# Weight prefetches of a mixture-of-experts stage issued from the SyncE queue instead of the ScalarE queue

## The reference, cut to what matters

```python
xn = _layernorm(x)
x = x + attn(xn) + ffn(xn)

# attn: one head of width 2048
qkv = einsum('bsh,oh->bso', xn, w_qkv) + b_qkv
q, k, v = split(qkv, 3)
probs = softmax(q @ k.T / sqrt(H))
out = (probs @ v) @ w_out.T + b_out

# ffn: 8 experts of width 1024, all computed densely, and a shared one
ht = rmsnorm(xn) ; top-2 of softmax(ht @ router_w) gives w_dense [t, 8]
eo = (silu(ht @ w_gate[e]) * (ht @ w_up[e])) @ w_down[e]
moe = sum over e of w_dense[:, e] * eo
sh  = (silu(ht @ sw_gate) * (ht @ sw_up)) @ sw_down
```

## Time and profile before

| | us |
|---|---|
| median of the 2 timed runs | 6501.62 |
| the 2 timed runs | 6351.88 and 6651.37 |
| the profiled execution | 6286.39 |
| span of its slowest core (core 2) | 6276.3 |
| spans of the 8 cores | 6231.8 to 6276.3 |
| PE busy | 4573.0 (73% of the span) |
| DVE busy | 1221.4 (19%) |
| ACT busy | 251.0 (4%) |
| POOL busy | 205.5 (3%) |

### The profile page before, as it was taken

How to read it: one execution, slowest core, us unless ns; L and a number is a source line. 1 busy time by engine, 2 the same in 40 slices (tenths; PEclk the granted TensorE clock), 3 DMA queues, 4 the chain that set the end, 5 groups by cost and what they waited for, 6 DMA issues and landing times.

```text
span 6276.3 us, 57133 instructions; the slowest of 8 cores (6231.8 to 6276.3 us)
## 1 busy us (share of the span) xinstructions
PE 4573.0 (73%) x20817; PEld 2015.4 (32%) x20817; DVE 1221.4 (19%) x2033; ACT 251.0 (4%) x404; POOL 205.5 (3%) x218
## 2 busy tenths in 40 slices
PE   0000000005999999999999999999967999989999
PEld 0000000002444344444444444444423444434433
DVE  2020110103131222212131312222121111112123
ACT  0000000000000000000000000000000000011000
POOL 1000000000000000000010000000000000000000
PEclk9555555556999999999999999999988999999999
DMA  9999999997795734536282735436295212133457
GB/s 131 121 125 119 127 120 126 120 110 177 184 206 118 111 64 87 94 62 114 40 141 41 125 56 96 81 75 107 46 119 80 70 36 59 56 110 92 117 165 221
DMA packets 730578, 666.60 MB, mean 106 GB/s; under 512 B 609016, under 2 KB 641816, under 8 KB 721728
## 3 DMA queue, kind: packets, MB, share of 16 engines
q0 software_dynamic: 51008, 314.77, 36.5%
q10 hardware_dynamic: 357408, 197.16, 12.9%
q1 hardware_dynamic: 321888, 151.03, 11.6%
HBM read 516.14 MB, written 390.07 MB: 144 GB/s over the span
## 4 chain that ended last, share of the span: by engine, by line
PE 64%; another core or an unknown queue 20%; DMA 10%; DVE 4%; issue 2%; DVEq 0%; ACTq 0%; ACT 0%; PEldq 0%; SPq 0%; PEld 0%; POOLq 0%
PE psA L482 16%; PE psA L490 16%; PE psB L547 9%; DMA moe_d<-jbuf 9%; PE psA L636 7%; PE psB L867 4%; PE psA L674 4%; PE psA L798 3%; PE psA L730 2%; PE psB L730 2%; DVE jbuf L557 1%; PE psA L639 1%; DVE mean L246 1%; DVE xn2ch L283 0%
## 5 line engine op out<-in xcount | busy, mean ns | idle before, releaser
L547 PE MATMUL psB<-wdb,a_s 128*128 128x512 bf16 x4608 | 1059.1, 393 | 149.6 <-DVEq L85 149.5
L482 PE MATMUL psA<-ht,wgb 128*128 128x512 bf16 x4608 | 1044.3, 380 | 1.0 <-DVEq L85 1.0
L490 PE MATMUL psA<-ht,wub 128*128 128x512 bf16 x4608 | 1041.6, 379 | 0.0
L300 PE MATMUL psA<-identb_s,xn2ch 128*128 128x128 bf16 x256 | 29.6, 305 | 1094.7 <-DVEq L85 1094.7
L547 PEld LDWEIGHTS psB<-wdb,a_s 128*128 128x128 bf16 x4608 | 459.0, 101 | 753.5 <-issue 257.4
L482 PEld LDWEIGHTS psA<-ht,wgb 128*128 128x128 bf16 x4608 | 451.4, 98 | 548.1 <-issue 6.2
L490 PEld LDWEIGHTS psA<-ht,wub 128*128 128x128 bf16 x4608 | 450.9, 98 | 543.7
L557 DVE COPY jbuf<-psB 128x512 f32<-128x512 f32 x576 | 398.5, 692 | 820.9 <-DMA moe_d<-jbuf 550.4
L636 PE MATMUL psA<-ht,wqp 128*128 128x512 bf16 x2048 | 465.5, 380 | 30.7 <-DMA bqh<-b_qkv 30.7
L506 DVE TENSOR_TENSOR tmul<-psA,wb 128x512 bf16<-128x512 f32 x256 | 177.2, 692 | 1447.1 <-PE psA L490 1447.1
L300 PEld LDWEIGHTS psA<-identb_s,xn2ch 128*128 128x128 bf16 x256 | 25.1, 140 | 1099.1 <-issue 1099.1
(11 more groups left out here) (91 smaller groups left out, 1251.0 us busy)
## 6 DMA issues: line engine op xcount, KB each, us to landing
moe_d<-jbuf POOLq DMA_DIRECT2D x144, 1024.0 KB, 10.1
wgb<-wg_bf ACTq DMA_DIRECT2D x72, 512.0 KB, 4.5
wub<-wu_bf ACTq DMA_DIRECT2D x72, 512.0 KB, 6.3
wdb<-wd_bf ACTq DMA_DIRECT2D x18, 2048.0 KB, 23.9
wg_bf<-w_gate POOLq DMA_DIRECT2D x8, 4096.0 KB, 555.6
wu_bf<-w_up POOLq DMA_DIRECT2D x8, 4096.0 KB, 595.2
wd_bf<-w_down POOLq DMA_DIRECT2D x8, 4096.0 KB, 635.6
wqkv_bf<-w_qkv POOLq DMA_DIRECT2D x12, 2048.0 KB, 675.1
```

The costliest lines, as they stand in the source:

```text
L482: last = en.matmul(pg[:, :], wgb[par][:, dc * 128:(dc + 1) * 128], self.ht[:, dc * T + tt * 512: dc * T + (tt + 1) * 512], start=(dc == 0) ...
L490: last = en.matmul(pu[:, :], wub[par][:, dc * 128:(dc + 1) * 128], self.ht[:, dc * T + tt * 512: dc * T + (tt + 1) * 512], start=(dc == 0) ...
L547: last = en.matmul(pj[:, :], a_s[:, fc * T + tc * 128: fc * T + (tc + 1) * 128], wdb[parj][:, fc * 1024 + dt * 512: fc * 1024 + (dt + 1) * ...
```

## The change

The two prefetch helpers of `p3_moe` name SP ("sync") instead of ACT ("scalar") as the engine that waits and issues. Where they are called in the code stays the same, and so do the buffers, the conditions waited for and the sizes.

```diff
         def prefetch_gu(e, fc, parity, after_te=0):
-            self.wait("scalar", "te", after_te)
-            self.wait("scalar", f"g_stgm{e}", self.stgm_done_e[e])
+            self.wait("sync", "te", after_te)
+            self.wait("sync", f"g_stgm{e}", self.stgm_done_e[e])
             wg_t[(e, fc)] = self.dma(
-                "scalar", f"c_wg{parity}",
+                "sync", f"c_wg{parity}",
                 wgb[parity][:, :].rearrange("p (dc f) -> p dc f", dc=ND),
                 self.d_wg_bf[e, :, fc * 128:(fc + 1) * 128]
                 .rearrange("(dc p) f -> p dc f", p=128))
             wu_t[(e, fc)] = self.dma(
-                "scalar", f"c_wu{parity}",
+                "sync", f"c_wu{parity}",
                 wub[parity][:, :].rearrange("p (dc f) -> p dc f", dc=ND),
                 self.d_wu_bf[e, :, fc * 128:(fc + 1) * 128]
                 .rearrange("(dc p) f -> p dc f", p=128))
 
         def prefetch_wd(e, half, parity, after_te=0):
-            self.wait("scalar", "te", after_te)
-            self.wait("scalar", f"g_stgm{e}", self.stgm_done_e[e])
+            self.wait("sync", "te", after_te)
+            self.wait("sync", f"g_stgm{e}", self.stgm_done_e[e])
             wd_t[(e, half)] = self.dma(
-                "scalar", f"c_wd{parity}",
+                "sync", f"c_wd{parity}",
                 wdb[parity][:, :].rearrange("p (fc d) -> p fc d", fc=NFC),
                 self.d_wd_bf[e, :, half * 1024:(half + 1) * 1024]
                 .rearrange("(fc p) d -> p fc d", p=128))
```

## The result

The changed kernel is slower: its time is 1.0441 times that of before, with a 95% interval of 1.0366 to 1.0516. On the lowest runs that is 6582.42 us against 6305.02. The medians of all runs, 6840.34 of 11 against 6642.28 of 10, hold executions of both kernels in which the cores of one half of the chip ran at a lower clock and some per cent longer; the ratio is made without them. The median of before has thus moved too, from the 6501.62 of the two first runs.

What follows compares the result with a forecast made beforehand. The prediction saw no bottleneck in ACT's queue; staging moved behind SP's last prefetch would start near 4488 us instead of 1416. +294 us of delay less 7 gained gave +287 on 6351.9, say 6640 us, range 6510 to 6900.

Steps and rivals of the forecast that it cites:

- the forecast 370: Ahead of the QKV projection: PE idle for about 370 us instead of 30.
- The rival by which only issue time moves: Staging still finishes in time, so the kernel's time stays within 2% at 6352 us; chance 0.03.
- The other-side rival: Expert 8's relieved down part gains 96 us, 106 with expert 0's; 6246 us if no tail over 106 remained; chance 0.02.
- the sum: Whole kernel: +294 us until the first load of wqkvT, less 7 gained in expert 0's down part, +287 us.
- the lower timed run: Base for the forecast time: 6351.9 us, the lower of two timed runs before the change; the other took 6651.4.
- the range: Forecast time of the whole changed kernel: 6510 to 6900 us.
- Nearer expert 0's 131: Expert 8's down part: 150 us taken between bounds 126 and 222, since expert 0 with staging beside it took 131.
- The pace of 23 us: Staging beside expert 8's down part: 6 steps at about 23 us each, from 22.9 beside expert 0's down part.
- the 222 us of before: Length taken for expert 8's down part before the change, with the xn_d transposes beside it; upper bound for after.
- 10 called the most: Expert 0's down part without staging: 131 us can fall at most 10, given 121.4 us of PE work; 7 taken.
- The clock: PE's lower clock after the longer idle gap before the projection: costs a few us at most, inside the error.
- The remark on the 150: Expert 8's down part length hardly matters: with 222 us the sum rises about 40, with 126 it falls 14.

## Why the prediction was right, and where it was not

**The reason was right.** The staging behind all prefetches in an in-order queue is the whole loss, shown by taking each part alone. That PE finds its weights as before (1.0 us of waits at L482), that the ACT queue gives nothing, and that the staging beside gate/up had cost nothing all came out so. PE's idle time ahead of the projection, 368.8 us for the forecast 370, is in part luck: both of its ends came some 40 us later than laid out. The rival by which only issue time moves was wrong, as its order of rows said. The other-side rival named a real collision, but its tail never came under its bound.

**The stated time was on the wrong base.** The step that failed is the one that put the sum on "the lower timed run". The sum said +287 us, 4.5% of 6352, and that change came out. The ratio of 1.0441 makes +280 of the same 6352, and the two profiled executions differ by 327. But the predicted 6640 stands beside the stated median of 6501.62, and against that it is a change of 138 us, 2.1%: less than half of the 4.4% that the runs showed. The working itself gave 6789 on the median. That median was the middle of two runs 300 us apart, as far as the whole effect. Taking the low one as base for the new time and leaving the old one high halved the forecast change. The measured median, 6840, lies in the range, near its upper end, because the range, unlike the stated time, left room for a high base.

**The terms**, against the first load of wqkvT at 5057.7 forecast and 5097.0 measured on the slowest core:
- start 4488 forecast, 4484.4 measured; 5 steps in the rest of gate/up, as forecast, at 11.1 us each (11.4 forecast).
- The down part of expert 8 was mis-sized, the largest error of a term: 150 us taken, 199 measured, and 6 steps beside it stretched to 36.2 us each (4540.00 to 4757.21) where 23 was taken. The forecast had this stretch end at 4691.7 and it ended at 4757.2, 65 us later. Three readings lie behind it. "Nearer expert 0's 131" failed because expert 0 only writes, and the run without accumulation shows that this makes the difference. The pace of 23 us mixed two kinds of step: of the 6 beside expert 0 only the first 2 were of wqkv, from 1741.92 to 1805.9, 32 us each, and the other 4, of the smaller wout, took 18.4 each. And the 222 us of before were not the down part alone: its last matmuls, in the row below, end at 4738.0, after 196 us, and the other 25 us passed until the first load of wqkvT.
- The cores differ here. In the changed kernel six of the eight took 152 to 166 us for this part and 511 to 522 us from its first matmul to the first load of wqkvT, where the forecast had 150 and 516 (4541.7 to 5057.7). Cores 3 and 5 took 204 and 199, and the slowest core sets the time.
- 21 quiet wqkv steps took 181.9 us, 8.7 each, for the 202 forecast: 20 less.
- 16 wout steps took 113.6 us for 109.
- The xn_d transposes took 44.3 us (5052.66 to 5096.95) for 55. The Trainium skill's 261 GB/s, which DMA: Bandwidth & Descriptors, Latency and other measured facts, gives for a transposing DMA with a non-contiguous middle dimension, would have made it 32, an estimate; 8.39 MB in 44.3 us is 189 GB/s, so the measurement decides against that figure here, with all 8 cores at work.
- These add up: +65 - 20 + 5 - 11 = +39.
- Expert 0's down part gained 13 us (129 to 116) where 7 was taken and 10 called the most. The bound came from PE's busy time, which itself shrank from 121.4 to 116.0, so it was no floor.
- The clock: the first 16 matmuls behind the gap took 5.43 us against 4.96. Nothing, as said.

The row of before for the 196 us (start, us):

```profile
4729.28 8.75 PE L547 MATMUL psB<-wdb,a_s 128*128 128x512 bf16 x32 [3.88 <-DVEq L85]
```

**The remark on the 150** said that what a longer down part costs is paid back in steps done. On most cores it was, as the run with the steps held back shows (medians 518 and 525 us). On the slowest it was paid back badly, since steps there ran at 36 us instead of 9.

## What to carry to other kernels

Moving a DMA to an idle-looking queue moves it ahead of everything that the code emits on that queue later: look not at how long the queue sleeps but at what stands behind the sleep, and at its due time. Work with slack belongs in small pieces between the prefetches, beside compute that leaves the DMA engines free, and away from stretches of accumulating DMAs. Of such a stretch read all cores, not one: the one that sets the time may be the exception. And state a forecast change and a forecast time on the same base.

## What the runs showed of the hardware

- Accumulating DMAs left little room for others. With the same 6 staging steps beside them, down parts took 179 us on average over the cores with accumulation (128 without steps) and 125 with plain writes of the same size (116 without steps), and the core moved 152 against 221 GB/s. Alone, an accumulated MB held all 16 DMA engines for 6.2 us, a written one for 2.6.
- Transposing loads were not much worse neighbours than plain loads of the same bytes: 179 against 166 us per down part on average over the cores, in one execution each.
- 16 transposes of 512 KB took 184 us beside accumulations and 45 alone, and a wait that keeps them apart makes the kernel 0.65% faster (interval 0.25% to 1.05%).
- A step of transpose, wait, write, wait takes 8.7 us on an otherwise idle core for 768 KB and 7.1 for 512 KB, with the DMA engines at 0.60: one at a time, such steps leave 40% of them idle. The 16 xn_d transposes of 512 KB, issued without waits between, took 2.8 us each.
